# Closing the second and third block's softmax denominators two steps later in an attention kernel

## The reference

```python
scores = jnp.einsum('bqhd,bkhd->bhqk', q, k)
scores = scores + jnp.einsum('bqr,bkr->bqk', q_rope, k_rope)[:, None]
scores = jnp.where(causal[None, None], -jnp.inf, scores / scale)
w = jax.nn.softmax(scores, axis=-1)
attn = jnp.einsum('bhqk,bkhd->bqhd', w, v).reshape(Bb, Tt, D_MODEL)
```

## Time and profile before

| | |
|---|---|
| median of 3 runs | 3612.92 us |
| profiled execution, and its span | 3614.76 us, 3613.0 us |
| TensorE (PE) busy | 3506.1 us, 97% |
| DVE, ACT, POOL busy | 2540.1, 1811.9, 2673.6 us |
| transfers on SP's queue | 423.10 MB |

### The profile page before, as it was taken

One profiled execution on the slowest core, in us unless ns is written; L12 is line 12 of the kernel. 1 busy time (PEld: TensorE's weight loads), 2 busy tenths in 40 slices (PEclk: granted clock), 3 DMA queues, 4 the chain that ended last, 5 costly groups with the idle time before them and its releaser, 6 DMA issues. The chain is left out here.

```text
span 3613.0 us, 54217 instructions
## 1 busy us (share of the span) xinstructions
PE 3506.1 (97%) x19552; PEld 2408.8 (67%) x19552; DVE 2540.1 (70%) x5329; ACT 1811.9 (50%) x3455; POOL 2673.6 (74%) x1194
## 2 busy tenths in 40 slices
PE   8999989999999999999999999999999699999999
PEld 4777756666666666666666666666665488888887
DVE  6676777777777777677777777777775366666665
ACT  2434335555555555555555555555555344444443
POOL 2333349889898898898988989889889566666665
PEclk9999989999999999999999999999999799999999
DMA  5778763463534535436346353463552111212120
GB/s 197 272 273 304 260 169 72 108 140 78 132 87 110 138 79 117 113 90 146 80 100 147 74 131 92 102 138 83 114 125 72 62 59 70 70 70 71 70 70 36
DMA packets 232756, 426.58 MB, mean 118 GB/s; under 512 B 25380, under 2 KB 26916, under 8 KB 232488
## 3 DMA queue, kind: packets, MB, share of 16 engines
q1 hardware_dynamic: 232424, 423.10, 43.2%
q10 hardware_dynamic: 64, 0.02, 0.0%
HBM read 300.86 MB, written 121.65 MB: 117 GB/s over the span
## 5 line engine op out<-in xcount | busy, mean ns | idle before, releaser
L1046 ACT ACTIVATE att_probs<-att_ps_s 128x512 f32<-128x512 f32 (+3 forms) x2560 | 1301.7, 536 | 938.7 <-PE att_ps_s L1207 850.1
L1146 POOL TENSOR_TENSOR att_sum_g<-att_sum_g,att_probs 128x2048 f32<-128x2048 f32 (+3 forms) x400 | 1626.0, 4065 | 72.8 <-ACT att_probs L1046 34.0
L1082 DVE TENSOR_REDUCE att_piece_max<-att_ps_m 128x1 f32<-128x512 f32 x1520 | 945.5, 681 | 136.1 <-PE att_ps_m L1190 134.2
L1206 PE MATMUL att_ps_s<-att_q_a,att_k_a 128*128 128x512 f32 (+3 forms) x2560 | 952.0, 374 | 17.2 <-DMA att_q_b<-att_neg_max 7.0
L1207 PE MATMUL att_ps_s<-att_q_b,att_k_b 65*128 65x512 f32 (+3 forms) x2560 | 934.6, 367 | 0.0
L1085 DVE CUSTOM_DVE_ANT_0 att_ps_m<-att_ps_m,mask_qk 128x128 f32<-128x128 f32 x1008 | 477.6, 508 | 268.2 <-PE att_ps_m L1190 254.9
L1190 PE MATMUL att_ps_m<-att_k_a,att_q_a 128*128 128x512 f32 (+3 forms) x1808 | 650.6, 384 | 5.9 <-DVE att_piece_max L1085 3.6
L1206 PEld LDWEIGHTS att_ps_s<-att_q_a,att_k_a 128*128 128x128 f32 x2560 | 486.1, 190 | 129.6 <-ACT att_probs L1046 42.5
L1213 PE MATMUL att_ps_o<-att_probs,att_v 128*32 128x512 f32 (+3 forms) x5120 | 546.8, 536 | 4.2 <-POOL att_probs L1126 4.2
L1207 PEld LDWEIGHTS att_ps_s<-att_q_b,att_k_b 65*128 65x128 f32 x2560 | 484.8, 189 | 65.7
L1190 PEld LDWEIGHTS att_ps_m<-att_k_a,att_q_a 128*128 128x128 f32 x1808 | 341.2, 190 | 225.0 <-issue 76.2
(11 more groups left out here) (189 smaller groups left out, 4955.8 us busy)
## 6 DMA issues: line engine op xcount, KB each, us to landing
att_q_a<-s_q_hi SPq DMA_DIRECT2D x128, 256.0 KB, 5.9
att_q_a<-s_qr_hi SPq DMA_DIRECT2D x128, 256.0 KB, 6.7
prj_x_sb<-in_x_dram SPq DMA_DIRECT2D x16, 1024.0 KB, 5.2
s_q_hi<-prj_q_hi SPq DMA_DIRECT2D x16, 1024.0 KB, 4.2
s_q_lo<-prj_q_lo SPq DMA_DIRECT2D x16, 1024.0 KB, 6.0
s_k_hi<-prj_k_hi SPq DMA_DIRECT2D x16, 1024.0 KB, 4.5
s_k_lo<-prj_k_lo SPq DMA_DIRECT2D x16, 1024.0 KB, 6.4
s_v<-prj_v_sb SPq DMA_DIRECT2D x16, 1024.0 KB, 9.1
```

The costliest lines, as they stand in the source:

```text
L1046: act.activation(probs[t % RING][:, hh, c0:CH], ps_s[(GH * t + hh) % SBANKS][:, c0:CH], ACT.Exp, scale=SCALE).then_inc(probs_ready, 1)
L1082: dve.tensor_reduce(top, ps_m[:, bank, :], AX_X, ALU.max).then_inc(piece_taken, 1)
L1146: pool.tensor_tensor(sum_g[:, :, c0:CH], sum_g[:, :, c0:CH], new, ALU.add).then_inc(sum_added, 1)
L1206: mm(out[:, c0:CH], k_a[:, hh, i * P:(i + 1) * P], q_a[j][:, hh, c0:CH], start=True, stop=False)
```

## The change

The closings of blocks 1 and 2 move from t = 13 and t = 25 to t = 15 and t = 27. Both stand behind the weighted values of that t, which are now the first two steps of the next block. The copy of the output sums out of `ps_o` by ScalarE (`take_output`) stays where it was (`TAKE_AT`). The inversions and `normalise` on DVE follow the closing: from 14, 15 to 16, 17, and from 26, 27 to 28, 29. The group of block 2 in `ps_d` was opened by its first step of ones before and is so now; it is ended by the closing now and not by the last step. `deal` puts the light pair where the inversions now are. Worked out by its formula, the numbers of pieces of maxima change as follows in every unit after the first (the first has the same change at steps 24 on, and a like one at 14 to 17):

| step | 12 | 13 | 14 | 15 | 16 | 17 | | 24 | 25 | 26 | 27 | 28 | 29 |
|---|---|---|---|---|---|---|---|---|---|---|---|---|---|
| before | 6 | 0 | 1 | 5 | 6 | 5 | | 5 | 1 | 0 | 6 | 6 | 6 |
| after | 6 | 5 | 6 | 0 | 1 | 5 | | 5 | 6 | 6 | 1 | 0 | 6 |

```diff
-ENDS_ON_PE = [owners[-1] == "T" for owners in SHARE_OF]
-OPENED_BY_SUM = ["T" not in owners.rstrip("T") for owners in SHARE_OF]
+CLOSE_LATER = (0, 2, 2, 0)
+CLOSES_FIRST = [owners[-1] == "T" and not later for owners, later in zip(SHARE_OF, CLOSE_LATER)]
+OPENED_BY_SUM = ["T" not in (owners.rstrip("T") if first else owners) for owners, first in zip(SHARE_OF, CLOSES_FIRST)]
...
-    closes = lambda m: CLOSING * any(FIRST[j] + 2 == 2 * m for j in range(TCH))
+    closes = lambda m: CLOSING * any((FIRST[j] + STEPS[j] + 2 + CLOSE_LATER[j]) % NSTEP == 2 * m for j in range(TCH))
...
-            if ENDS_ON_PE[j]:
+            if CLOSES_FIRST[j]:
                 return pv_done, NSTEP * u + FIRST[j] + STEPS[j] + RING
...
-        CLOSE_AT = {NSTEP * u + FIRST[j] + STEPS[j] - 1 + LAG: (u, j) for u in range(NU) for j in range(TCH)}
+        TAKE_AT = {NSTEP * u + FIRST[j] + STEPS[j] - 1 + LAG: (u, j) for u in range(NU) for j in range(TCH)}
+        CLOSE_AT = {t + CLOSE_LATER[j]: (u, j) for t, (u, j) in TAKE_AT.items()}
...
-                if t in CLOSE_AT:
-                    take_output(*CLOSE_AT[t])
+                if t in TAKE_AT:
+                    take_output(*TAKE_AT[t])
...
-                    last = over_keys(ps_d, ones, probs[s % RING], start=first, stop=(i == STEPS[j] - 1), c0=c0)
+                    last = over_keys(ps_d, ones, probs[s % RING], start=first, stop=(CLOSES_FIRST[j] and i == STEPS[j] - 1), c0=c0)
...
-                last = over_keys(ps_d, ones, sums[j % 2], start=opens, stop=not ENDS_ON_PE[j])
+                last = over_keys(ps_d, ones, sums[j % 2], start=opens, stop=not CLOSES_FIRST[j])
...
-                if closing and ENDS_ON_PE[closing[1]]:
+                if closing and CLOSES_FIRST[closing[1]]:
                     close_denominators(*closing)
                 for due in (t - LAG - 1, t - LAG):
                     weighted_values(*STEP_OF[due])
-                if closing and not ENDS_ON_PE[closing[1]]:
+                if closing and not CLOSES_FIRST[closing[1]]:
                     close_denominators(*closing)
```

## The result

The changed kernel takes 3658.62 us (median of 4 runs, 3657.21 to 3665.48) against 3612.78 us: a ratio of 1.0133 (95% interval 1.012 to 1.0145; the brackets behind later ratios are such intervals). It is 1.3% slower, where 0.4% was forecast; the range ended at 3646. The profiled execution took 3665.48 us (span 3663.7), 6.9 us above the median, so its own sums come out that much larger. Its mean granted clock was 0.981, that of the other three 0.983: by an estimate from these two (0.002 of 3664 us) the clock accounts for most of the 6.9 us.

The account below looks back on a forecast made before the run. TensorE, busy 97% of the span, was taken as the bound. From the profiled 3614.8 us: -25.2 (stalls), -2.8 (maxima), +31.5 (late keys), +11.6 (clock) = 3629.9, so 3628 us against the median 3612.9; range 3590 to 3646 us.

Parts of the forecast that it names:

- the clock: TensorE's granted clock falls to 1.2 GHz behind 7 of 15 stalls: +11.6 us, bounds 0 and 24.8.
- The stop: TensorE waits in step 33 for late keys, 2.1 us in each of 15 units: +31.5 us.
- the gain: Waits for POOL at the closings of blocks 1 and 2 go, -25.2 us; fewer bank waits, -2.8 us.
- The store and the queue behind it: Block 2's store on SP moves later, with key and v loads queued behind it, so the second quarter's keys land late.
- K: Start of the first load of the second quarter of keys, after the scores of step 31; the store's times count from it.
- step 5 of that part: TensorE stops in step 33 for 2.0 to 2.2 us, taken as 2.1; bounds 0 and 2.9.
- the relief by DVE: Maxima dealt anew, so TensorE waits less for a bank behind block 2's inversions: -0.2 us in 14 units, -2.8 us.
- The last unit: Bound by POOL in block 3; gains the idle time POOL loses behind the slow step 25, 1.97 us.
- Rival 1: Keys late in step 33 but the clock stays up: 3616.5 us, no change; chance 0.18.
- rival 2: Keys come in time or nearly: 3585 us without a stall, 3600 with one of 1.0 us; chance 0.27.
- rival 3: Closing finds POOL late again, or ACT its ring tile unsummed: no gain, 3653 us; chance 0.10 with the rest.
- The forecast's own range: Whole kernel: 3612 us (stall 1.8 us, two falls) to 3645 us (stall 2.5 us, eleven falls).

Follow-up runs that it names:

- e1: Changed kernel with block 2's output store moved behind the next unit's first quarter of keys and v: 3593.74 us, ratio to the kernel before 0.9949.
- e8: Kernel before, with only its first quarter of keys held until the first head's scores of step 30: 3677.47 us, ratio 1.0185.
- e6: Changed kernel with block 2's store issued behind the first of the six loads of keys: 3629.76 us, ratio to the kernel before 1.0047.
- e7: Changed kernel with block 2's store issued behind the first two loads of keys: 3599.11 us, ratio to the kernel before 0.9966.
- e5: Changed kernel with nine extra matmuls before TensorE's wait for the second quarter of keys in step 33: 3633.54 us, ratio to the kernel before 1.0061.
- e2: Kernel before with the closing of block 1 alone moved (CLOSE_LATER 0, 2, 0, 0): 3603.8 us, ratio 0.9977.
- e4: Kernel before with only block 2's output store moved behind the first quarter of keys and v: 3613.36 us, ratio 1.0001.
- e9: e1 with the maxima dealt out as in the kernel before: 3649.27 us, ratio to the kernel before 1.0105.

## Why the prediction was wrong in size

The mechanism, its place and its direction were as forecast. The step that failed most is the clock: 11.6 us in the sum, and 24.8 as its upper bound, where the profiled execution lost about 32. The stop (31.5 us, measured 43) and the gain (28 us, measured 22) were mis-sized the same way.

1. **The store and the queue behind it: right, to 0.1 us in a quiet unit.** The store at K - 5.8 (said K - 5.7), the normalising 5.6 us into step 29, v directly behind the keys, the keys landing at K + 9.4 in the unit shown (said K + 9.3). e1 and e8 show it from both sides, e6 and e7 the pace.
2. **The stop, step 5 of that part: 2.87 us in the mean, not 2.1**, so 43 us and not 31.5. In six of 15 units it was 2.1 to 2.4 as worked out, in four of them (units 6 to 9) 3.5 to 4.3. I had read the landing time from one quiet unit and rounded down, while the late piece of the earlier trace rows already said that the same transfer can take 1.8 us longer (7.0 against 5.2; DMA issues of the kernel before, 1488 to 1491.5):

```profile
att_k_a<-s_kr_lo SPq DMA_DIRECT2D x1, 256.0 KB, 7.0
```

   My upper bound was 2.9, and the mean lies just under it.
3. **The clock: the largest miss.** I took 7 falls at 1.65 us, 11.6 us, with 24.8 as the most. There were 14, and six lasted 6.8 us: 68 us at 1.2 GHz. The excess of step 33 beyond the stops, 5.0 - 2.87 = 2.1 us in 15 units, is 32 us, and half of the 68 us is 34; e5 gives 25 us back with the fill, its own stops and one fall left. The median run had less of it than the profiled one (granted clock 0.983 against 0.981). The bound was too low since it took every fall for as long as the one seen.
4. **The gain: 1.35 us per unit and not 1.66 + 0.2.** The stalls themselves are gone. Block 1's steps gave 0.78 us of the 0.88. Of block 2's 0.78 us about 0.27 came back in step 26, 3.42 us with six pieces (step 28 before had the same pieces and 3.14): the relief by DVE that I counted at -0.2 was not there. The last unit gained 2.8 us and not 1.97, since it had the wait at block 1's closing too (0.63 us by the profile, at 2741, past the end of the window of the earlier trace rows). That window starts behind the first unit's closings as well, so it could not show that they had no wait; the whole trace shows none, and my count of 14 units was right by luck. Together 21.7 us by the lengths instead of 28; e1 measures 18, with an interval of 13 to 25.

Sum for the profiled execution with the measured terms: 3614.8 - 19 (14 x 1.35) - 3 (last unit, 129.5 to 126.7 us) + 43 + 32 = 3668, against 3665.5. Rival 1 (no fall) failed at the clock, rival 2 (keys in time) at the queue's pace, rival 3 found nothing late at POOL. The forecast's own range was added up wrongly too: a stall of 1.8 us with two falls gives 3615 us and not 3612, and 2.5 us with eleven falls 3641 and not 3645; neither reaches what was measured. The 358 GB/s of the Trainium skill, "DMA: Bandwidth & Descriptors", Specifications, are not reached: a full queue moved 235 GB/s here (the last section's window).

## What to carry to other kernels

Before an instruction is moved, follow what its result releases on the in-order queue of transfers, and count every load queued behind that wait, with 1.15 us per 256 KB here; the wait lists of the kernel before show nothing of it while there is 0.6 us to spare. Price a stop of TensorE of 2 us or more at its length and at a fall of the clock besides (here 32 us beside 43 us of stops), and take stops from the worst unit as well as the quiet one. A store that nobody waits for belongs behind the loads that somebody does.

## What the runs showed of the hardware

- Longer stops brought the clock down more often, but no length decides it: in e7 no stop of up to 1.5 us did and one of 1.61 us did, in e6 one of 2.49 us did not, and of the 15 stops of 2.1 us and more in the changed kernel 14 did; the one that did not was 2.73 us long. Nor does the length tell how long the clock stays down: the four longest stops there (3.5 to 4.3 us) were followed by 3.4 us at 1.2 GHz, and six of 2.2 to 2.9 us by 6.8 us. What decides between these was not tried and stays open. Nine matmuls inside the stop kept the clock at 2.4 GHz in 14 of 15 units.
- A transfer can land late though the queue runs at full pace. In units 3 and 8 of the changed kernel (the first is unit 0) the windows over the queue show the same rate, 235 and 234 GB/s, and 183 and 191 over the next 4.6 us; yet the last `k_a` transfer took 8.1 and 10.0 us (the windows, then two issues of unit 8):

```profile
1056.00:1066.00 10.00, 10.00 (x51) 6.33 (x51) 8.81 (x16) 5.36 (x10) 9.27 (x3) 1.00 1.05 235
1807.50:1817.50 10.00, 10.00 (x51) 6.34 (x50) 8.81 (x16) 5.36 (x10) 9.27 (x3) 1.00 1.07 234
```
```profile
att_k_a<-s_kr_lo SPq DMA_DIRECT2D x1, 256.0 KB, 10.0
att_k_b<-s_k_hi SPq DMA_DIRECT2D x1, 256.0 KB, 9.6
```

The keys of unit 8 and the load issued 0.47 us behind them landed within 0.1 us (1822.1); in unit 3 the keys landed 1.3 us ahead of it. Units 6 to 9 are late ones in five of the six kernels that queued five or more loads behind the store or held them (not in e5). Unit 6 is late without such a queue as well, by 1.2 to 1.7 us in the kernel before, e1, e2, e4 and e9, and unit 7 in e1 by 0.8 us. Why these units was not tried and stays open.
